# A transformer layer on one core: four setup banks, later bias products, and unused products in the setup

## The reference, cut to what matters

```
x = x + self_attention(layernorm(x))          # 16 heads of 16 features, biases on q, k, v
x = x + cross_attention(layernorm(x), ctx)    # 16 heads of 64 features, ctx is 64 rows per input
x = x + ffn(layernorm(x))                     # router (entmax over 16 experts), two low-rank products, GELU
```

## Time and profile before

| what | us |
|---|---|
| three runs | 1010.55, 1012.16, 1015.98 (median 1012.16) |
| the profiled execution, its own time | 1011.2 |
| its span, first to last instruction | 1009.4 |
| PE busy / DVE busy / ACT busy / POOL busy | 961.7 / 766.3 / 587.5 / 148.8 |
| mean granted TensorE clock | 0.99 of full speed |

### The profile page before, as it was taken

The page is one execution under the profiler, slowest core; times in us unless marked ns, Lnnn a source line. Parts: engine busy times, 40 slices in busy tenths (PEclk is TensorE's granted clock), DMA queues, the critical chain, the costliest instruction groups (busy, mean ns, idle before and its releaser), DMA issues.

```text
span 1009.4 us, 15848 instructions
## 1 busy us (share of the span) xinstructions
PE 961.7 (95%) x5238; PEld 577.6 (57%) x5238; DVE 766.3 (76%) x1610; ACT 587.5 (58%) x837; POOL 148.8 (15%) x177
## 2 busy tenths in 40 slices
PE   5879999999999999999999999999999999998998
PEld 4434444556556665566556655665566654565777
DVE  3566756897899769987898779876998689737874
ACT  2436767655467565756566655756575556764533
POOL 2000000013012200221021211220022102211320
PEclk9889999999999999999999999999999999999999
DMA  6487786743320215120441126021602043005001
GB/s 172 109 269 230 239 263 200 229 107 116 82 68 2 64 48 157 49 64 2 130 121 36 27 69 182 7 57 53 177 22 63 15 141 76 1 10 160 0 1 43
DMA packets 77930, 97.38 MB, mean 96 GB/s; under 512 B 10383, under 2 KB 60370, under 8 KB 76850
## 3 DMA queue, kind: packets, MB, share of 16 engines
q1 hardware_dynamic: 77874, 96.69, 33.7%
HBM read 41.41 MB, written 29.36 MB: 70 GB/s over the span
## 4 chain that ended last, share of the span: by engine, by line
PE 72%; DVE 13%; SPq 5%; ACT 3%; issue 3%; DMA 2%; POOL 0%; POOLq 0%; DVEq 0%; ACTq 0%
PE y_ps L984 23%; PE x_ps L984 17%; PE pv_ps L984 9%; PE sm_ps L984 8%; PE st_ps L984 8%; DVE mx L1628 4%; PE y_ps L1147 3%; SPq L832 2%; ACT probs L1421 2%; PE y_ps L1113 1%; DMA xa<-in_x 1%; DMA q_st<-nm 1%; SPq L908 1%; DVE stat L1648 1%; PE x_ps L1075 1%
## 5 line engine op out<-in xcount | busy, mean ns | idle before, releaser
L1628 DVE TENSOR_REDUCE mx<-sm_ps 128x2 f32<-128x1024 f32 x256 | 312.0, 1219 | 98.4 <-PE sm_ps L984 97.3
L1421 ACT ACTIVATE probs<-st_ps 128x1024 f32<-128x1024 f32 x256 | 262.2, 1024 | 188.5 <-PE st_ps L984 183.0
L984 PE MATMUL pv_ps<-probs,v_all 128*32 128x512 f32 x1024 | 132.4, 604 | 0.4 <-ACT o_t L1421 0.4
L984 PE MATMUL sm_ps<-k_st,q_st 50*128 50x512 f32 x512 | 122.8, 472 | 4.6 <-DVE mx L1628 2.1
L984 PE MATMUL st_ps<-q_st,k_st 52*128 52x512 f32 x512 | 120.2, 464 | 4.1 <-ACT probs L1421 2.3
L984 PE MATMUL x_ps<-b_cat,pt 128*128 128x256 f32 x448 | 110.2, 386 | 0.0
L984 PEld LDWEIGHTS sm_ps<-k_st,q_st 50*128 50x128 f32 x512 | 48.9, 185 | 88.4 <-issue 42.7
L984 PEld LDWEIGHTS x_ps<-b_cat,pt 128*128 128x128 f32 x448 | 80.9, 190 | 20.8 <-issue 9.9
L984 PEld LDWEIGHTS st_ps<-q_st,k_st 52*128 52x128 f32 x512 | 48.5, 184 | 67.5 <-issue 30.9
L699 POOL TENSOR_TENSOR px<-px,cst 128x512 f32<-128x512 f32 x56 | 57.9, 1045 | 197.0 <-DVE cst L1723 196.8
L984 PE MATMUL y_ps<-a_cat,xt_hi 128*128 128x512 f32 x232 | 77.8, 417 | 0.3 <-DVE xt_lo L1618 0.2
(11 more groups left out here) (304 smaller groups left out, 1693.2 us busy)
## 6 DMA issues: line engine op xcount, KB each, us to landing
a_scr<-a_cat SPq DMA_DIRECT2D x16, 1024.0 KB, 5.8
a_cat<-a_scr SPq DMA_DIRECT2D x8, 2048.0 KB, 8.8
q_st<-qk_hi SPq DMA_DIRECT2D x128, 64.0 KB, 2.2
k_st<-qk_hi SPq DMA_DIRECT2D x128, 64.0 KB, 2.2
b_scr<-b_cat SPq DMA_DIRECT2D x8, 1024.0 KB, 5.1
b_cat<-b_scr SPq DMA_DIRECT2D x16, 512.0 KB, 11.1
xa<-in_x SPq DMA_DIRECT2D x9, 512.0 KB, 4.3
q_st<-qk_lo SPq DMA_DIRECT2D x64, 64.0 KB, 2.2
```

The costliest lines, as they stand in the source:

```text
L984: return nc.tensor.matmul(dst, lhs, rhs, start=start, stop=stop, **kw)
L1421: return nc.scalar.activation(dst, src, f, **kw)
L1628: nc.vector.tensor_reduce(mx[:, c % 2, 0:16].rearrange("p (m x) -> p m x", m=2)[:, :, col], sm_ps[:], axis=AX, op=ALU.max).then_inc(sm_tak ...
```

## The change

1. **Four banks.** The first 34 setup units of `EARLY_PE` (those ahead of the first `P`, an even number; `HEAD`) take four banks in turn: y_ps 1, st_ps 0, y_ps 0, st_ps 1, with a semaphore of its own for each (`head_taken`). The first `P` waits until the last of these units on either st bank has been read.
2. **Bias.** TensorE's bias products and ACT's reading of them move behind the transposes of input 0 and ACT's copies of these.
3. **Unused products.** DVE zeroes a corner of `xo` at its very start. TensorE multiplies this corner with itself (fp32, 128 by 128 by 128) and nobody reads the results: 14 times at the very start, twice after each `setup_w`, four times after the bias, and twice at each of 14 places `WU` in `EARLY_PE`, after every fourth or so entry. `WU` 0 to 2 write `sm_ps`, `WU` 3 on write `pv_ps`.

The rest of `EARLY_PE`, and all other tables, are as before. Counters of later units on `y_taken` are lowered by the 34 units that no longer use it.

```diff
 EARLY_PE = (
-    (0, "SW", 0, 0), (-2, "SW", 0, 0), (-2, "SW", 1, 0), (-2, "SW", 2, 0), (-2, "SW", 3, 0), (-2, "SW", 4, 0),
...
+    (0, "SW", 0, 0), (-2, "SW", 0, 0), (-2, "SW", 1, 0), (-2, "SW", 2, 0), (0, "WU", 0, 0), (-2, "SW", 3, 0),
+    (-2, "SW", 4, 0), (-2, "SW", 5, 0), (-2, "SW", 6, 0), (0, "WU", 1, 0), (-2, "SW", 7, 0), (-2, "SW", 8, 0),
+    (-1, "SW", 0, 0), (-1, "SW", 1, 0), (0, "WU", 2, 0), (-1, "M", 16, 0), (0, "SW", 1, 0), (-1, "M", 17, 0),
+    (0, "SW", 2, 0), (0, "WU", 3, 0), (-1, "M", 18, 0), (0, "SW", 3, 0), (0, "SW", 4, 0), (-1, "M", 19, 0),
+    (0, "WU", 4, 0), (0, "SW", 5, 0), (0, "SW", 6, 0), (-1, "M", 20, 0), (1, "SW", 2, 0), (0, "WU", 5, 0),
+    (0, "SW", 7, 0), (-1, "M", 21, 0), (0, "SW", 8, 0), (1, "SW", 0, 0), (0, "WU", 6, 0), (-1, "M", 22, 0),
+    (0, "SW", 9, 0), (0, "SW", 10, 0), (-1, "M", 23, 0), (0, "WU", 7, 0), (1, "SW", 1, 0), (-1, "M", 24, 0),
+    (1, "SW", 3, 0), (1, "SW", 4, 0), (0, "WU", 8, 0), (-1, "TN", 3, 0), (-1, "M", 25, 0), (1, "SW", 5, 0),
+    (1, "SW", 6, 0), (0, "WU", 9, 0), (0, "X1", 0, 0), (-1, "M", 26, 0), (1, "SW", 7, 0), (1, "SW", 8, 0),
+    (0, "WU", 10, 0), (-1, "M", 27, 0), (2, "SW", 1, 0), (1, "SW", 9, 0), (-1, "M", 28, 0), (0, "WU", 11, 0),
+    (1, "SW", 10, 0), (-1, "M", 29, 0), (0, "P", 0, 0), (2, "SW", 0, 0), (0, "WU", 12, 0), (0, "X1", 1, 0),
+    (2, "SW", 3, 0), (-1, "M", 30, 0), (2, "SW", 2, 0), (0, "WU", 13, 0), (0, "P", 2, 0), (-1, "M", 31, 0),
...
+HEAD_BANKS = 4
+HEAD = 2 * (sum(u[1] == "SW" for u in EARLY_PE[:[u[1] for u in EARLY_PE].index("P")]) // 2)
...
+WARM = 14
+WARM_LATE = sum(u[1] == "WU" for u in EARLY_PE[:[u[1] for u in EARLY_PE].index("M")])
...
+        def s_bank(u):
+            if head_turn(u):
+                return (y_ps[:, 1], st_ps[:, 0], y_ps[:, 0], st_ps[:, 1])[head_turn(u)[1]]
+            return y_ps[:, u % 2]
...
         def s_fill(pe, u):
-            wait(pe, y_taken[u % 2], u // 2)
-            return y_ps[:, u % 2]
+            if head_turn(u):
+                turn, k = head_turn(u)
+                if turn > 0:
+                    pe.wait_ge(head_taken[k], turn)
+                elif k % 2 == 0:
+                    pe.wait_ge(y_taken[1 - k // 2], 2 + k // 2)
+                else:
+                    pe.wait_ge(qk_taken, 1 + k // 2)
...
                     wait(pe, exp_done, b.times(STEPS, e // 2))
+                    if is_first(b) and e == 0:
+                        head_end(pe, 1)
+                        head_end(pe, 3)
...
+            def warm(bank, n):
+                for _ in range(n):
+                    mm(bank[:, 0:P], xo[:, 0, 0:P], xo[:, 0, 0:P], True, True)
+
             first = At(None, 0)
+            pe.wait_ge(warm_tile, 1)
+            warm(sm_ps[:, 1], WARM)
             pe.wait_ge(const_ready, CONSTS)
             pe.wait_ge(qk_in, 16 * 5)
             for n in range(4):
                 setup_w(n)
-            setup_bias()
+                warm(sm_ps[:, 1], 2)
             for k in range(KT):
                 turn_x1(first, k)
+            setup_bias()
+            warm(sm_ps[:, 1], 4)
             for j in range(4):
                 qk(first, j)
...
+                elif kind == "WU":
+                    if i == WARM_LATE:
+                        pe.wait_ge(qk_taken, 4)
+                    warm(sm_ps[:, 1] if i < WARM_LATE else pv_ps, 2)
...
-            run(bqkv[:], s_filled(act, SU_BIAS)[:, 0:6]).then_inc(y_taken[SU_BIAS % 2], 1)
             for k in range(KT):
                 x1_hi(first, k)
+            run(bqkv[:], s_filled(act, SU_BIAS)[:, 0:6]).then_inc(y_taken[SU_BIAS % 2], 1)
...
             first = At(None, 0)
+            nc.vector.memset(xo[:, 0, 0:P], 0.0).then_inc(warm_tile, 1)
             dve.wait_ge(qk_in, 16 * 5)
```

More of the change, by code:

```diff
@@ L502, in build_kernel @@
         small = sem("small")
+        warm_tile = sem("warm_tile")
         c_clear = sem("c_clear")
@@ L545, in build_kernel @@
         y_taken = [sem("y_taken0"), sem("y_taken1")]
+        head_taken = [sem(f"head_taken{n}") for n in range(HEAD_BANKS)]
         tail_taken = [sem(f"tail_taken{n}") for n in range(TAIL_BANKS)]
@@ L602, in order @@
             return SETUP_UNITS + before + len(PLAN) * (g.off - 2) + n
-        early = [(u[0], u[2]) if u[1] == "SW" else u[1:3] for u in EARLY_PE if u[1] not in X_BANK and u[3] == 0]
+        early = [(u[0], u[2]) if u[1] == "SW" else u[1:3] for u in EARLY_PE if u[1] not in X_BANK + ("WU",) and u[3] == 0]
         def setup_no(p, n):
@@ L641, in fill @@
                 elif k < 2:
-                    pe.wait_ge(y_taken[k], (before_tail() - k + 1) // 2)
+                    pe.wait_ge(y_taken[k], (before_tail() - HEAD - k + 1) // 2)
                 elif k < 4:
@@ L647, in fill @@
                 return y_of(g, kind, i)
+            if g.reg is None and n < SU_EARLY + HEAD + 2:
+                head_end(pe, 2 * (1 - n % 2))
             for u in after:
@@ L650, in fill @@
                     taken(pe, g, *u)
-            wait(pe, y_taken[n % 2], nth(g, n // 2, len(PLAN) // 2))
+            wait(pe, y_taken[n % 2], nth(g, (n - HEAD) // 2, len(PLAN) // 2))
             return y_ps[:, n % 2]
@@ L666, in taken @@
                 return
-            eng.wait_ge(y_taken[n % 2], nth(g, n // 2 + 1, len(PLAN) // 2))
+            eng.wait_ge(y_taken[n % 2], nth(g, (n - HEAD) // 2 + 1, len(PLAN) // 2))
         def split(g, i):
@@ L754, in w_unit, with head_turn, head_end, s_done @@
             return n if n < 4 else setup_no(-2, IN_W + n - 4)
-        def s_fill(pe, u):
-            wait(pe, y_taken[u % 2], u // 2)
-            return y_ps[:, u % 2]
+        def head_turn(u):
+            return divmod(u - SU_EARLY, HEAD_BANKS) if SU_EARLY <= u < SU_EARLY + HEAD else None
+        def head_end(eng, k):
+            wait(eng, head_taken[k], (HEAD - k + HEAD_BANKS - 1) // HEAD_BANKS)
+        def s_bank(u):
+            if head_turn(u):
+                return (y_ps[:, 1], st_ps[:, 0], y_ps[:, 0], st_ps[:, 1])[head_turn(u)[1]]
+            return y_ps[:, u % 2]
+        def s_done(u):
+            return head_taken[head_turn(u)[1]] if head_turn(u) else y_taken[u % 2]
+        def s_fill(pe, u):
+            if head_turn(u):
[6 more added lines that the diff above has]
+                    pe.wait_ge(qk_taken, 1 + k // 2)
+            elif u < SU_EARLY:
+                wait(pe, y_taken[u % 2], u // 2)
+            elif u < SU_EARLY + HEAD + 2:
+                wait(pe, y_taken[u % 2], (u - HEAD) // 2)
+                head_end(pe, 2 * (1 - u % 2))
+            else:
+                wait(pe, y_taken[u % 2], (u - HEAD) // 2)
+            return s_bank(u)
         def s_filled(eng, u):
             eng.wait_ge(y_full, u + 1)
-            return y_ps[:, u % 2]
+            return s_bank(u)
         def s_taken(eng, u):
-            eng.wait_ge(y_taken[u % 2], u // 2 + 1)
+            if head_turn(u):
+                turn, k = head_turn(u)
+                eng.wait_ge(head_taken[k], turn + 1)
+            else:
+                eng.wait_ge(y_taken[u % 2], (u - (HEAD if u >= SU_EARLY else 0)) // 2 + 1)
         def in_chunk_order(ap):
@@ L1373, in setup_unit @@
                 if n >= 7 and (n - 7) % 2 == 1:
-                    banks = (y_ps[:, setup_no(p, n - 1) % 2], y)
+                    banks = (s_bank(setup_no(p, n - 1)), y)
                     for i in range(2):
@@ L1553, in setup_unit @@
                     elif n == IN_O2:
-                        run(wout2_t[:], y[:, 0:D]).then_inc(y_taken[u % 2], 1)
+                        run(wout2_t[:], y[:, 0:D]).then_inc(s_done(u), 1)
                     else:
-                        save_v(y, y_taken[u % 2], At(None, 0), n - IN_V)
+                        save_v(y, s_done(u), At(None, 0), n - IN_V)
                     return
                 if p < 0:
-                    run(ctx_t[:, n, :], y).then_inc(y_taken[u % 2], 1)
+                    run(ctx_t[:, n, :], y).then_inc(s_done(u), 1)
                     return
-                done = y_taken[u % 2]
+                done = s_done(u)
                 if n == 0:
@@ L1957, in setup_unit @@
                     cols = slice(N * (n - IN_O1), N * (n - IN_O1) + N)
-                    lo_part(wout1_lo[:, cols], y_ps[:, u % 2], wout1_hi[:, cols]).then_inc(y_taken[u % 2], 1)
+                    lo_part(wout1_lo[:, cols], s_bank(u), wout1_hi[:, cols]).then_inc(s_done(u), 1)
                     return
@@ L1964, in setup_unit @@
                 dst, hi = (a_cat[:, :, m, part, XD * j:XD * j + XD] for part in (1, 0))
-                lo_part(dst, y_ps[:, u % 2].rearrange("p (b s) -> p b s", b=B), hi).then_inc(y_taken[u % 2], 1)
+                lo_part(dst, s_bank(u).rearrange("p (b s) -> p b s", b=B), hi).then_inc(s_done(u), 1)
             def iteration(b):
@@ L1990, in w_lo_part @@
                 dve.wait_ge(w_hi_done, n + 1)
-                y, dst, hi = y_ps[:, u % 2, 0:D], w_lo[:, n // 2, n % 2, :], w_hi[:, n // 2, n % 2, :]
```

(4 more changed lines are left out.)

## The result

The changed kernel took **1017.88 us** (median of 22 runs, 1012.11 to 1024.8); the kernel before, run beside it, took 1013.86 (22 runs, 1010.3 to 1019.33). The ratio is **1.0038**, 95% interval 1.0023 to 1.0053: slower by 0.4%. The prediction was 1010.5 us against a median of 1012.16, a ratio of 0.9984, with a range up to 1013.6. So the difference is less than the half per cent that I had called "no change", but it goes the other way, and the time lies outside the range.

What follows compares the result with a forecast made beforehand. TensorE is busy 95% of the span, so only its waits and lower clock, ahead of 85 us, can give time back. 1.6 + 0 + 1.9 - 1.1 - 0.8 = 1.6 us earlier: 1010.5 us against 1012.16, range 1005.0 to 1013.6.

Steps and rivals of the forecast that it cites:

- up to M16: Setup up to the first `M` (M16): gain 1.6 us, between -1.6 and 4.0, M16 at 38.9 instead of 40.50.
- M16 to the landing of the second store: From the first `M` on: 0, between -2.5 and 2.5; bank waits go, six blocks come, mostly becoming DVE waits.
- to the first `P`: From the `M` behind the second store to the first `P`: loss 1.1 us, between 0.3 and 1.9.
- The store step: At pair 0's second store: four banks let the next `M` follow DVE's reduction, gain 1.9 us, between 0 and 2.5.
- the wait of `P`: Ahead of the first `P`: new wait of 1.0 us until ACT's `b_cat` copies have read both st banks.
- The clock may fall again: PE idle some 2.5 us until 65.7; a clock fall would cost 1.6 us more, half of it, 0.8, counted.
- The start: Warm-up, bias and `qk`: 0; the 14 products run while PE waits for loads, and DVE stands until 29.77 us.
- Two blocks ahead of M16: Ahead of the first `M`: four unused products at 0.25 us each, 1.0 us at the upper clock level.
- Behind the first `P`: After the first `P`: two blocks where PE is nearly full, loss 0.8 us, between 0 and 1.0.
- The unused products lie on the path: Slower rival: from `WU` 1 on, 26 products delay `M` entries DVE waits for, 6.5 us, 1018.7 us; chance 0.06.
- The level holds: Faster rival: PE at the upper clock by 31 us and no fall at 65, gain 5.5 us, 1006.7 us; chance 0.27.
- Its own sign of being wrong: At the first `P`: the prediction called itself wrong if it came later than 76.9 us.

Runs made afterwards that it cites:

- experiment 3: Changed kernel with 32 instead of 34 setup units on the four banks, all unused products kept: 1014.68 us, ratio 1.0013 to the kernel before.
- experiment 1: Changed kernel without any of its 54 unused products; four banks and moved bias stay: 1011.09 us, ratio 0.9965 to the kernel before.
- experiment 9: Changed kernel without the `WU` blocks, the start's 26 unused products kept, input 1's load ahead of the mask-row transfers: 1013.66 us, ratio 0.9999.
- experiment 5: Changed kernel without the 26 unused products of the start; the 28 of the `WU` blocks stay: 1012.37 us, ratio 0.9981.
- experiment 11: Changed kernel with only `WU` 8 to 11 of the unused products, input 1's load first, 32 units on four banks: 1008.18 us, ratio 0.9946.
- experiment 10: Changed kernel with two banks and no unused products, so only the moved bias is left: 1014.29 us, ratio 0.9999.
- e2_two_banks: Changed kernel with two banks as before; moved bias and all 54 unused products stay: 1019.77 us, ratio 1.0049.
- experiment 7: Changed kernel without unused products, input 1's load ahead of the 12 mask-row transfers on SP's queue: 1010.75 us, ratio 0.9964.
- experiment 8: Changed kernel without unused products, input 1's load ahead of the mask-row transfers, 32 setup units on the four banks: 1010.1 us, ratio 0.9956.
- experiment 12: Changed kernel keeping only the 14 unused products at the very start; four banks and moved bias stay: 1012.6 us, ratio 0.9972.
- experiment 4: Changed kernel with all unused products, input 1's load ahead of the 12 mask-row transfers on SP's queue: 1015.33 us, ratio 0.9995.
- experiment 6: Changed kernel without the `WU` blocks; the 26 unused products of the start stay: 1013.9 us, ratio 0.9990.

## Why the prediction was wrong, step by step

The shift of the profiled run after against the one before, cut at the prediction's steps (minus is earlier):

| step | forecast | measured | from |
|---|---|---|---|
| up to M16 | -1.6 | -0.1 | 40.40 - 40.50 |
| M16 to the landing of the second store | 0 | +1.2 | 24.96 - 23.72 |
| landing to the next `M` | -1.9 | -1.9 | 3.10 - 5.02 |
| to the first `P` | +1.1 | +1.9 | 9.54 - 7.63 |
| first `P` to 183 us | +0.8 | +0.5 | 104.99 - 104.50 |
| 183 to 209 us | 0 | +2.3 | 26.03 - 23.78 |
| 209 us to the last output store | 0 | +3.0 | 803.85 - 800.81 |

- **The store step held.** The next `M` follows DVE's reduction 3.1 us behind the landing (forecast 3.05), and 1.92 us are gained (forecast 1.9). So did the wait of `P`: forecast 1.0, found 1.17, and experiment 3 shows that it costs all of it. "The clock may fall again" held too: the wait ahead of that `M` was forecast at 2.5 us and was 2.34. The store itself landed at 65.36, not at 62.6.
- **The banks were priced right.** The sum had 1.8 us for the unused products (1.0 ahead of M16, 0.8 behind the first `P`). Without them it gives 1.6 + 1.8 = 3.4 us, a ratio of 0.9966; experiment 1 measured 0.9965, and M16 came at 37.75, where 38.9 less 1.0 is 37.9.
- **The step that failed is the price of the unused products:** 1.8 us forecast, 6.8 measured between the changed kernel and experiment 1. The two profiles show where, up to the first `P`, 4.05 us apart:
  - *The start, put at 0:* the statistics come 31.35 - 29.64 = 1.71 later. DVE's standstill was to cover the start; I didn't ask what sets its end, SP's issue of the load. Counted from the statistics, M16 was forecast at 38.9 - 29.77 = 9.13 us and came at 9.05, so that step missed by the late load alone. And experiment 9 shows that the load is not the whole cost of the start.
  - *Two blocks ahead of M16, put at 1.0:* 9.05 - 8.11 = 0.94.
  - *Six blocks behind M16, put at 0:* they did turn into waits. From M16 to the store `SA 0 0` it is 9.25 us, against 9.24 in experiment 1, although three of the blocks lie in the chain. But the second store lands another 0.96 later, with the long SP issue.
  - *Three blocks between `TN` and the first `P`, `WU` 9 to 11:* the sum has no term for them. Two lie in the chain (1.15 and 0.64); with the longer wait of `P` the stretch takes 9.54 - 9.09 = 0.45 more.
  - *Behind the first `P`, put at 0.8:* 0.63 up to 183 us (104.99 against 104.36), and then a part that no step foresaw (below).
- **A block cost what I took it for at the upper clock:** 0.44 to 0.64 us in the chain, forecast 0.5. At the lower it took 0.85 and 1.15.
- **A reading was wrong without effect.** Two of the six waits that were counted as waits for a bank are waits for ACT's copies that the product reads (`px`, 0.26, and `xt_f`, 0.35), so 1.9 us could go and not 2.5; the step was put at 0 anyhow.
- **The rival that came true had the wrong working.** "The unused products lie on the path", chance 0.06, gave 1018.7, 1.0065 of its median; the measured 1.0038 is on its side. But it let the blocks carry the whole loss, each by delaying an `M`, and by experiment 5 they alone cost 1.3 us, a fifth of that.
- **"The level holds" did not come.** PE stood for 7.08 us with no product in between, and the clock was 0.61 up to M16 (0.65 before). The Trainium skill, page "TensorE: Matmul & The Clock Gate", section "HAM oscillation — how this bites in real kernels", advises for products with few rows to restructure the loop, so that TensorE stays warm, or to pad the rows. The unused products, another kind of padding with the same aim, held the level behind the store in experiment 5 (clock 1.00), not in the changed kernel or in experiment 11 (0.88 in both), and in the changed kernel they cost more than they gave. The same section of the Trainium skill's page reports of another kernel that double-buffered PSUM brought no further gain; that does not carry over to this one, where the banks alone turn a ratio of 0.9999 into 0.9965 (experiments 10 and 1).
- **Its own sign of being wrong came.** The first `P` was to come no later than 76.9, and came at 78.00.

**Where the rest went.** Behind 183 us the two kernels run the same instructions, and the changed one loses 5.3 us more in these two profiles. Of this, 2.3 are seen on one chain of the changed kernel:

```profile
179.78 1.94 SPq L877 DMA_DIRECT2D q_st<-qk_lo  x1
...
187.55 0.51 SPq L837 DMA_DIRECT2D xa<-in_x  x1
...
191.67 0.43 DVE L1708 BATCH_NORM_STATS2 stat<-xa 128x6 f32<-128x256 f32 x1 [1.86 <-DMA xa<-in_x]
...
193.28 0.49 PE L1029 MATMUL sm_ps<-k_st,q_st 50*128 50x512 f32 x2 [1.66 <-DVE mx L1688]
```

One SP issue takes 1.94 us instead of 0.59, the next input is loaded that much later, DVE waits 1.86 for it, PE 1.66 for DVE, and the clock falls (0.83 from 195 to 205). In `e2_two_banks` the issue of another pair of transfers took 2.78 there, and PE waited 1.93; in `e5_blocks_only` one took 2.03 and PE waited 1.71. In experiments 1, 3 and 7 to 12 no such issue was long, DVE waited 0.50 to 1.04 and PE under 1 us; experiments 4 and 6 lie between (DVE 1.30 and 1.26, PE 1.07 and 1.03), 6 without a long issue. Another 1.2 us are the end: from the store of an output at 934.72 to the last at 1012.87 it is 78.15 us, against 76.98 before, with the clock at 0.69 from 940 to 950. The rest is spread.

**What stays open.** That the unused products cost 7 us is shown, and that both halves cost more than either alone. That together they cost more than the sum of both is not. Some long SP issues go with the products: between 53 and 60 us, all four kernels with all 54 (the changed one, experiments 2 to 4) have one transfer to `q_st` or `k_st` that takes 1.23 to 1.49 us to issue where it takes 0.59 in the ten others. Why the issues are long is not known. One profile was taken of each kernel, and runs of one kernel lie up to 10 us apart, so how much of the 5.3 us behind 183 us is due to the products, and how, stays open; by the medians it is some 2 us (6.8 less the 4.68 seen up to 183).

## What to carry to other kernels

A product that nobody uses can be free only where its engine waits longer than the product takes, and where whatever ends that wait can't be delayed by it: read both before adding it, block by block, and give every block a term (three had none here). Even then it can cost, if the clock falls at a place where nothing covers it, as in experiment 9. Take the parts of a bundled change singly; here the four banks gained a third of a per cent, the moved bias nothing, and the unused products took back twice the gain. And where a buffer lets an engine run ahead into a wait that another engine ends, the gain at that wait is the work that lay behind it, no more: here it could be worked out from two rows (1.9 forecast, 1.92 measured). It need not last: 1.5 us of it were gone at the first `P`, and what stayed of the banks' gain was made earlier, ahead of M16.

## What was unexpected of the hardware

- The spread between runs of one kernel follows the mean granted clock. In the 35 runs of the kernel before that stood beside experiments 1 to 4, the fastest took 1010.61 us at 0.992 and the slowest 1020.94 at 0.982. Between these two that is about 1 us for each 0.001, so runs that differ by 10 us need not have done different work. Whether the clock makes the time or longer waits make both is not shown.
- A wait of PE of 1.5 to 1.7 us can keep the clock or lose it. In a wait of 1.53 us before it fell, and behind 1.66 at 193.28 in the changed kernel; through 1.51 in `e5_blocks_only` (ahead of its `M` at 66.22) and through 1.71 there (ahead of its `M` at 190.62) it stayed at 1.00.
- SP's issue of one same-sized transfer takes 0.59 us in most places and 1.1 to 2.0 in a few, some of them the same in every kernel, some at other places in other kernels. In a setup that hangs on SP's order, one of them moves everything behind it.
